# Scan stage of a GCN and Mamba kernel: VectorE's small steps between a slot's product and its scans

## The reference, cut to what matters

```
x = x + L0(relu(layernorm(x)))          # relu(adj_norm @ h @ W.T + b)
h = relu(layernorm(x))
h = relu(adj @ h @ gcn_w + gcn_b);  h = layernorm(h) * ln_g + ln_b
xc, z = split(h @ w_in);  u = silu(conv(xc) + conv_b)
dbc = u @ w_xp;  dt = softplus(dbc[:, :8] @ w_dt + b_dt);  B, C = dbc[:, 8:24], dbc[:, 24:]
state = exp(dt * A) * state + dt * B * u        # per row, 256 x 16 states
y = state @ C + u * D_skip;  out = (y * silu(z)) @ w_out
x = x + out
```

## Time and profile before

| what | value |
|---|---|
| median of 3 runs | 2611.35 us (2610.81 to 2611.61) |
| the profiled execution's own time | 2612.32 us |
| its span, first to last instruction | 2610.5 us |
| mean granted TensorE clock | 0.947 of full speed |
| VectorE busy, whole span | 2085.1 us (80%) |
| TensorE busy, whole span | 2222.9 us (85%) |
| GpSimd busy, whole span | 1067.6 us (41%) |
| ScalarE busy, whole span | 978.6 us (37%) |
| first product of the scan stage starts | 1464.4 us |

### The profile page before, as it was taken

One profiled execution on the slowest core, in us unless ns is written; L12 is line 12 of the kernel. 1 busy time (PEld: TensorE's weight loads), 2 busy tenths in 40 slices (PEclk: granted clock), 3 DMA queues, 4 the chain that ended last, 5 costly groups with the idle time before them and its releaser, 6 DMA issues.

```text
span 2610.5 us, 21684 instructions
## 1 busy us (share of the span) xinstructions
PE 2222.9 (85%) x6736; PEld 1251.9 (48%) x6736; DVE 2085.1 (80%) x2087; ACT 978.6 (37%) x1696; POOL 1067.6 (41%) x461
## 2 busy tenths in 40 slices
PE   0436889999999999999999988889988988886776
PEld 0212334444457888888885434444444443443333
DVE  7899998888527656656652599999999999999997
ACT  0100000000015555555551455555555555555552
POOL 0000000000000000000000499999999999998554
PEclk9968899999999999999999989999999999997898
DMA  9999999989756556555556656665656565562221
GB/s 393 417 421 422 421 418 387 391 360 381 276 214 237 207 201 225 189 215 201 198 181 243 240 202 220 207 215 214 214 204 227 206 223 194 215 210 69 69 73 53
DMA packets 108322, 642.99 MB, mean 246 GB/s; under 512 B 14224, under 2 KB 15024, under 8 KB 42672
## 3 DMA queue, kind: packets, MB, share of 16 engines
q1 hardware_dynamic: 92160, 604.02, 61.4%
q10 hardware_dynamic: 16048, 37.57, 4.0%
HBM read 625.28 MB, written 16.25 MB: 246 GB/s over the span
## 4 chain that ended last, share of the span: by engine, by line
PE 55%; DVE 24%; DMA 8%; issue 8%; ACT 4%; DVEq 0%; ACTq 0%; SPq 0%
PE ps L848 21%; PE ps L767 14%; PE ps L888 10%; DVE ps L685 6%; DVE arena L590 6%; DMA ring<-adj 5%; DVE arena L700 5%; PE ps L966 4%; DVE ring L700 3%; DMA arena<-adj 2%; PE ps L917 2%; PE ps L909 1%; PE ps L970 1%; DVE parts L726 1%; PE ps L928 1%
## 5 line engine op out<-in xcount | busy, mean ns | idle before, releaser
L458 POOL TENSOR_TENSOR rstd<-base,minus_half 128x8 f32<-128x8 f32 (+1 forms) x40 | 84.7, 2118 | 1406.4 <-DVE base L510 811.7
L848 PE MATMUL ps<-adj_parts,h_parts 128*128 128x512 f32 x2592 | 593.6, 390 | 2.6 <-ACT adj_parts L1062 2.2
L888 PE MATMUL ps<-ring,diag_h 128*128 128x512 f32 x1152 | 566.2, 627 | 0.9 <-DVE arena L672 0.9
L848 PEld LDWEIGHTS ps<-adj_parts,h_parts 128*128 128x128 f32 x2592 | 484.7, 188 | 109.0 <-ACT adj_parts L1062 4.7
L590 DVE TENSOR_TENSOR arena<-arena,ring 128x2048 f32<-128x2048 f32 x180 | 412.6, 2292 | 57.9 <-DMA ring<-adj 47.2
L767 PE MATMUL ps<-ring,arena 128*128 128x512 f32 x824 | 381.9, 622 | 53.1 <-DMA ring<-adj 53.0
L474 POOL TENSOR_TENSOR arena<-arena 128x1024 f32<-128x1024 f32 x156 | 377.6, 2431 | 67.7 <-ACT state L1129 67.6
L700 DVE TENSOR_TENSOR_SCAN arena<-arena,state,ps 128x512 f32<-128x512 f32 x312 | 382.4, 1267 | 28.6 <-ACT arena L1137 8.7
L888 PEld LDWEIGHTS ps<-ring,diag_h 128*128 128x128 f32 x1152 | 229.5, 201 | 254.1 <-issue 248.9
L609 DVE TENSOR_TENSOR adj_parts<-ring,adj_parts 128x1024 fp32r<-128x1024 f32 x216 | 264.0, 1225 | 94.5 <-ACT adj_parts L1062 83.7
L1137 ACT ACTIVATE arena<-arena,a_sb 128x512 f32<-128x512 f32 x512 | 338.4, 708 | 0.4
(11 more groups left out here) (97 smaller groups left out, 2095.5 us busy)
## 6 DMA issues: line engine op xcount, KB each, us to landing
ring<-adj SPq DMA_DIRECT2D x452, 1024.0 KB, 6.6
arena<-c_scratch SPq DMA_DIRECT2D x128, 512.0 KB, 4.2
diag_h<-adj SPq DMA_DIRECT2D x32, 1024.0 KB, 12.6
arena<-adj SPq DMA_DIRECT2D x28, 1024.0 KB, 16.1
arena<-x ACTq DMA_DIRECT2D x16, 512.0 KB, 6.0
x_scratch<-arena ACTq DMA_DIRECT2D x8, 512.0 KB, 3.0
arena<-x_scratch ACTq DMA_DIRECT2D x16, 256.0 KB, 5.4
out<-arena ACTq DMA_DIRECT2D x16, 256.0 KB, 3.7
```

What stands on the lines that cost most here:

```text
L848: last = nc.tensor.matmul(acc[:, c, :], h_parts[:, blk % 2, layer, h_part, a * F:(a + 1) * F], adj_parts[:, buf, adj_part, c * MM:(c + 1) ...
L888: last = nc.tensor.matmul((acc_c if i else y_ps)[:, c, :], tile_of(h1, JT * s + a), blk[:, a * STRIP + c * MM:a * STRIP + (c + 1) * MM], s ...
```

## The change

The block of small steps in VectorE's loop is moved, unaltered, from behind the two scans to in front of them: behind the product and ahead of the wait for the decays. The scans get their own `if`, since the steps also run in slots without scans; there nothing changes. No other engine's program changes. Cut to its core (the diff's moved lines are the steps from BIAS to RESIDUAL, here with their waits):

```diff
                     nc.vector.tensor_tensor(dbu_ps[g % 2], w[k % 2],
                                             b_ps[g % 2].unsqueeze(1).to_broadcast([P, HALVES, T]), ALU.mult)\
                         .then_inc(dbu_done, 1)
+                k = chunk_at(g, BIAS)
+                if k is not None:
+                    dve.wait_ge(misc_full, misc_at["gcn", k] + 1)
...
+                k = chunk_at(g, STATS)
+                if k is not None:
+                    dve.wait_ge(normed, NORM_C + k)
+                    dve.wait_ge(relu_done, k + 1)
+                    norm_stats([gbuf[:, t, :] for t in range(CT)])
+                k = chunk_at(g, NORMALISE)
+                if k is not None:
+                    norm_bias(CT)
+                k = chunk_at(g, SPLIT)
+                if k is not None:
+                    dve.wait_ge(bc_high, k + 1)
...
+                k = chunk_at(g, WEIGHTED_U)
+                if k is not None:
+                    dve.wait_ge(dt_ready, k + 1)
+                    dve.wait_ge(u_ready, k + 1)
...
+                k = chunk_at(g, SKIP)
+                if k is not None:
+                    dve.wait_ge(nsum_done, sums(k, DS - 1))
...
+                k = chunk_at(g, GATE)
+                if k is not None:
+                    dve.wait_ge(y_free, k + 1)
+                    dve.wait_ge(sz_ready, k + 1)
...
+                k = chunk_at(g, RESIDUAL)
+                if k is not None:
+                    dve.wait_ge(misc_full, misc_at["out", k] + 1)
+                    dve.wait_ge(x1t_in, 16 * (k + 1))
...
+                if 0 <= g < NCH * DS:
+                    k, n = divmod(g, DS)
                     dve.wait_ge(da_ready, g + 1)
...
                     dve.wait_ge(dbu_done, g + 1)
                     for h in range(HALVES):
                         nc.vector.tensor_tensor_scan(hs[g % HSB][:, h, :], da[g % 2][:, h, :], dbu_ps[g % 2][:, h, :],
                                                      state[:, h, n:n + 1], ALU.mult, ALU.add).then_inc(scan_done, 1)
-
-                k = chunk_at(g, BIAS)
-                if k is not None:
...
```

More of the change, by code:

```diff
@@ L687, in _ @@
                         .then_inc(dbu_done, 1)
[L688 to L701, removed]
                 k = chunk_at(g, BIAS)
@@ L754, in _ @@
                         .then_inc(misc_free, 1)
+                if 0 <= g < NCH * DS:
+                    k, n = divmod(g, DS)
+                    dve.wait_ge(da_ready, g + 1)
+                    if k:
+                        dve.wait_ge(state_saved, g - DS + 1)
+                    if g >= HSB:
+                        k_old, n_old = divmod(g - HSB, DS)
+                        if k_old < QUAD_CHUNKS and n_old % 4:
+                            dve.wait_ge(quad_done, (g - HSB) // 4 + 1)
+                        else:
+                            dve.wait_ge(nsum_done, sums(k_old, n_old))
+                    dve.wait_ge(dbu_done, g + 1)
+                    for h in range(HALVES):
+                        nc.vector.tensor_tensor_scan(hs[g % HSB][:, h, :], da[g % 2][:, h, :], dbu_ps[g % 2][:, h, :],
+                                                     state[:, h, n:n + 1], ALU.mult, ALU.add).then_inc(scan_done, 1)
         @block.tensor
```

## The result

The changed kernel takes 2629.39 us (median of 6, 2627.44 to 2631.37), the kernel before 2611.44 (median of 6). The ratio is 1.0067 with a 95% interval of 1.0055 to 1.0078: **18.0 us slower**. The prediction was 2626. TensorE's and ScalarE's instructions stand two lines lower than before (L909 is now L911, L928 L930, L938 L940, L947 L949, L987 L989). VectorE's steps have new lines: BIAS L695, SPLIT L712, WEIGHTED_U L720, SKIP L727, GATE L734, RESIDUAL L739, the scans L755.

What follows compares the result with a forecast made beforehand. VectorE was taken as the bound, TensorE in n=4 to 9, with GpSimd just behind. Terms +29.0 - 23.0 + 4.7 + 4.4 + 2.6 - 2.7 - 0.4 gave +14.6 us, so 2626 us, range 2612 to 2640.

Steps and rivals of the forecast that it cites:

- the two large terms: 29.0 us lost at n=9 and 23.0 us gained at n=13 to 15; n is the slot's number in its chunk.
- the loss at n=9: Slot 9 of a chunk: RESIDUAL waits for TensorE's output product with the scans queued behind it; 29.0 us lost over 15 occurrences.
- the gain at n=13 to 15: Last three slots of a chunk: BIAS frees the PSUM bank sooner, the decays' wait goes; 23.0 us gained over 14 chunks.
- Steps that meet GpSimd: Moved steps may wait for a running GpSimd operation: SPLIT 4.4 us lost, GATE and WEIGHTED_U together 2.6.
- SPLIT's +4.4: SPLIT starts earlier but still waits for the same GpSimd add: 0.4 us lost per chunk, in 11 chunks 4.4.
- the hidden gap: A step behind the product hides the gap before the scans, 0.21 us per slot; at n=1, 2.7 us gained in 13 chunks.
- GATE and WEIGHTED_U: GATE of the last chunk, WEIGHTED_U of the one before: each meets the GpSimd operation the scans released, losing 1.3 us.
- SKIP, +4.7 predicted: n=4 in the last two chunks before the tail: both scans come behind SKIP's wait for its sum, 2 x 2.37 us lost.
- No change: Rival: GpSimd and TensorE run ahead during the n=9 stop, SPLIT and GATE meet no operation; 2613.4 us, chance 0.17.
- GpSimd decides for the worse: Rival: SPLIT meets a GpSimd operation at its start and waits 2.35 us instead of 0.75; 2641 us, chance 0.13.
- the rival "faster": Rival: moved steps fall between GpSimd's operations, so SPLIT's and GATE's waits on it come back; 2600 us, chance 0.08.

## Why the prediction was right, point by point

The sign and the size (18.0 us slower against 14.6 by the sum) hold, and so do the two large terms, each by itself. That the loss at n=9 outweighs the gain at n=13 to 15 holds only for the whole stage, by 27.4 against 24.1, and explains 3.3 of the 18 us; in chunks 0 to 12 it is 23.8 against 26.9. That the sum came out so near is in part luck, since two errors of opposite sign cancel. Split at chunk 13, the sum's terms are about +4.9 for chunks 0 to 12 and +9.6 for 13 to 15; the traces show -3.4 and +18.2. Nor does one place alone make the kernel slower: it is no slower than before with RESIDUAL put back (0.9995), nor with the old order in the last three chunks (0.9988).

**RESIDUAL, 29.0 predicted.** n=9 shows +27.4; alone it is +28.6. The waits before it sum to 32.5 us over 15 chunks; 2 to 3 us were announced for nearly all of them and came in ten. Right.

**BIAS and the end of the chunk, -23.0 predicted.** n=13 to 15 show -24.1: -26.9 in chunks 0 to 12, +2.2 in chunk 13 and +0.7 in chunk 14. BIAS waits 0.4 us, TensorE 0.9 for it, no scan waits for decays: right in mechanism. The term was too small in the full chunks, because STATS's L510 shortened from a mean of 805 to 354 ns: RESIDUAL's stop lets GpSimd come level, so the step meets only the last 0.3 us of its add in most chunks. With RESIDUAL put back that is lost again (1508 ns). Gain and loss are thus not independent, which the sum took them to be. The prediction also gave the gain to the whole group of three steps; BIAS alone carries it.

**Steps that meet GpSimd.** SPLIT's +4.4 was mis-sized: n=11 shows +0.9 in chunks 0 to 12. SPLIT lasts 1543 ns on average in chunks 1 to 12, 1251 before, and the hidden gap of 0.21 pays for most of that; the phase read from one chunk did not repeat. GATE is the same story: 2204 ns for 1656, which uses up what n=4 gains. The 2.7 us for the hidden gap at n=1 did not come: it is +1.7 in chunks 0 to 12. NORMALISE's instruction (L514) takes 856 ns on average in chunks 1 to 12, 597 before, which cancels the 0.21; in chunks 0 and 14 it loses 1.3 each, which makes +3.0 at n=1 in all. These two losses are the very mechanism that the prediction priced for GATE and WEIGHTED_U and did not apply to NORMALISE: behind the product it meets the operation which the scans before released. VectorE's timeline, then GpSimd's, chunk 14:

```profile
2466.01 1.67 DVE L514 SCALAR_TENSOR_TENSOR nmr<-mv,rstd 128x4 f32<-128x4 f32 x1
```

```profile
2465.30 2.36 POOL L474 TENSOR_TENSOR arena<-arena 128x1024 f32<-128x1024 f32 x1 [1.36 <-ACT state L1131]
```

It ends at 2467.68 and the operation at 2467.66; before it took 0.14. GATE lost 1.28 in the last chunk and WEIGHTED_U 0.66 in the one before, of the 1.3 each. Such pairs agree with the Trainium skill ("SBUF — State Buffer", Who interferes with whom), by which whichever of the two engines issues first blocks the other. The rule tells who waits; how often, only the phase of the traces told.

**SKIP, +4.7 predicted; and what the sum lacked.** The two late SKIPs cost 4.06 and 2.36, 6.4 together. The second is the predicted 2.37. The first is larger by 1.7, the length by which the pair sum grew at the lowered clock. The same left-out term is most of what SPLIT loses in chunk 14 (+3.5) and BIAS in chunk 13 (+3.9 at n=13). The sum also lacked 3.3 us of gain at n=6 and n=8; no run looked at those. **The step that failed** is that the prediction kept TensorE's late times as the earlier trace rows show them. There TensorE has idle time, so a stop of VectorE becomes an idle stretch of TensorE, the granted clock falls, and the next sum is late while VectorE stands waiting in front of its scans.

**The rivals.** No change fell with 18 us. That GpSimd decides for the worse did not happen in this kernel (2641 was its price), nor the gain. But the remark against the rival "faster", that GpSimd's sums then hold the chunk up, is what the kernel with RESIDUAL put back shows: 2610 instead of some 2602.

## What to carry to other kernels

A step goes ahead of long independent work only where its release is what another engine waits for (here BIAS, 14.5 us), and stays behind it where its own input comes late in the same slot (here RESIDUAL, 28.6 us; BIAS's input comes in its slot too, but cost it only 0.4 us of waiting): move one step at a time, not the block. Before gains are added up, ask which engine holds the stretch next; here GpSimd had 1.4 us of room in a chunk and took back 8 of 27 us, visible as longer instructions and not as waits. Where an engine's idle time is being used as the buffer, look at the granted clock as well as at the idle time.

## What the runs showed of the hardware

- Two VectorE instructions on 128x4 elements took 0.14 us (L514) and 0.17 us (L510) where no GpSimd operation was running, in the kernel before. In all other chunks of that kernel and in all of the changed one they ended 0.02 to 0.03 us behind the GpSimd operation that was running, after up to 1.67 and 1.97 us; the profile shows that wait inside their length, not as a wait. Scans, which read one operand from PSUM, took 1265 ns on average in the changed kernel and 1267 before.
- Taking a tenth off GpSimd's work made the kernel before 8 us slower (2620.27); in its trace NORMALISE's L514, which met another operation, accounts for 5.5.
- TensorE's granted clock was 1.00 from 2465.00 to 2477.60 us, in which the engine was busy for 6.85 of 12.60 us and stood still for the last 2.80, and 0.68 over the sum that followed. Which part of what went before makes it fall was not settled.
